# An image loaded and its statistics taken inside the filter stage; the next statistics taken inside the local convolution

## The reference, cut to what matters

```python
def _gn(v, G=8, eps=1e-05):
    g = v.reshape(B_, H_, W_, G, C_ // G)
    m = jnp.mean(g, axis=(1, 2, 4), keepdims=True)
    s = jnp.var(g, axis=(1, 2, 4), keepdims=True)
    return ((g - m) / jnp.sqrt(s + eps)).reshape(v.shape)

x = x + _L0_conv_ref(_gn(x), L0_conv_h0, L0_conv_numerators, L0_conv_denumerator)   # long filters, by FFT
x = x + _L1_conv_ref(_gn(x), ...)                                                   # 8x8 patches, large products
x = x + _L2_conv_ref(_gn(x), L2_conv_filters, L2_conv_bias)                         # 3x3 convolution
x = x + _L3_conv_ref(_gn(x), L3_conv_h0, L3_conv_numerators, L3_conv_denumerator)   # long filters again
```

## Time and profile before

| what | us |
|---|---|
| three runs: lowest, median, highest | 3507.69, 3509.49, 3510.06 |
| the profiled execution, its own time | 3497.7 |
| its span, first to last instruction | 3495.9 |
| TensorE busy | 3244.6 (93%) |
| VectorE busy | 1568.7 (45%) |
| ScalarE busy | 1680.7 (48%) |
| POOL busy | 1257.6 (36%) |

### The profile page before, as it was taken

The page is one execution under the profiler, slowest core; times in us unless marked ns, Lnnn a source line. Parts: engine busy times, 40 slices in busy tenths (PEclk is TensorE's granted clock), DMA queues, the critical chain, the costliest instruction groups (busy, mean ns, idle before and its releaser), DMA issues. The chain is left out here.

```text
span 3495.9 us, 82613 instructions
## 1 busy us (share of the span) xinstructions
PE 3244.6 (93%) x37272; PEld 2672.4 (76%) x37272; DVE 1568.7 (45%) x1926; ACT 1680.7 (48%) x1763; POOL 1257.6 (36%) x1018
## 2 busy tenths in 40 slices
PE   7999999589998699999899999999989997799998
PEld 6999998379998566666688776666668773489998
DVE  6787877411111434444765444344665444411112
ACT  3666665356553344444554434444454440355551
POOL 6888886055552102222440001222271000165550
PEclk9999999899999899999999999999999998899999
DMA  0333334787777321222133331222222344777776
GB/s 18 114 116 118 122 122 140 215 209 197 198 196 183 106 94 66 79 73 75 70 109 97 109 121 62 83 73 73 73 73 73 91 126 87 176 204 202 203 202 163
DMA packets 259721, 428.86 MB, mean 123 GB/s; under 512 B 28263, under 2 KB 106601, under 8 KB 257897
## 3 DMA queue, kind: packets, MB, share of 16 engines
q1 hardware_dynamic: 244346, 396.86, 38.9%
q10 hardware_dynamic: 15024, 26.72, 2.4%
HBM read 306.07 MB, written 113.77 MB: 120 GB/s over the span
## 5 line engine op out<-in xcount | busy, mean ns | idle before, releaser
L138 PE MATMUL m_bank<-xn,w 128*128 128x512 f32 x1536 | 619.2, 403 | 31.8 <-DVE m_store L1597 11.7
L139 PE MATMUL m_bank<-xn,w 128*128 128x512 f32 x1536 | 603.1, 393 | 0.0
L140 PE MATMUL m_bank<-xn,w 128*128 128x512 f32 x1536 | 602.8, 392 | 0.0
L774 PE MATMUL c_acc<-c_shifted,filt 128*32 128x256 f32 (+8 forms) x11264 | 457.2, 317 | 9.5 <-issue 9.4
L774 PEld LDWEIGHTS c_acc<-c_shifted,filt 128*32 128x32 f32 x11264 | 442.7, 159 | 20.3 <-issue 16.9
L568 POOL TENSOR_TENSOR filt<-filt 64x1408 f32<-64x1408 f32 x64 | 259.6, 4056 | 473.1 <-DMA filt<-filters_dram 473.1
L581 ACT ACTIVATE filt<-filt 64x2048 f32<-64x2048 f32 (+3 forms) x256 | 422.6, 1754 | 14.3 <-DMA filt<-filters_dram 10.6
L138 PEld LDWEIGHTS m_bank<-xn,w 128*128 128x128 f32 x1536 | 291.3, 190 | 172.9 <-issue 76.0
L129 ACT ACTIVATE w<-raw_weights 128x2048 fp32r<-128x2048 f32 x96 | 373.0, 3886 | 103.3 <-PE m_bank L140 102.0
L133 DVE TENSOR_TENSOR w<-raw_weights,w 128x2048 fp32r<-128x2048 f32 x86 | 334.0, 3883 | 159.0 <-ACT w L129 159.0
L140 PEld LDWEIGHTS m_bank<-xn,w 128*128 128x128 f32 x1536 | 291.1, 190 | 62.9
(11 more groups left out here) (182 smaller groups left out, 6763.7 us busy)
## 6 DMA issues: line engine op xcount, KB each, us to landing
c_shifted<-spectrum_dram SPq DMA_DIRECT2D x256, 270.0 KB, 3.9
filters_dram<-f_stage SPq DMA_DIRECT2D x128, 512.0 KB, 3.6
filt<-filters_dram SPq DMA_DIRECT2D x240, 256.0 KB, 4.7
raw_weights<-in_L_conv_Wq SPq DMA_DIRECT2D x16, 2048.0 KB, 8.7
raw_weights<-in_L_conv_Wk SPq DMA_DIRECT2D x16, 2048.0 KB, 8.6
raw_weights<-in_L_conv_Wv SPq DMA_DIRECT2D x16, 2048.0 KB, 8.6
m_qf<-in_L_conv_Wout SPq DMA_DIRECT2D x128, 256.0 KB, 3.9
spectrum_dram<-c_shifted SPq DMA_DIRECT2D x116, 136.0 KB, 2.4
```

The source lines that it names most:

```text
L138: pe.matmul(out, w[0], x[0], start=first, stop=False)
L139: pe.matmul(out, w[0], x[1], start=False, stop=False)
L140: return pe.matmul(out, w[1], x[0], start=False, stop=last)
L774: mm = nc.tensor.matmul(acc[k % 2][phase][32 * s:32 * s + 32, 0:B, LAGS * kb:HALF], filt[:, k, phase, :, :, 4 * kb + s].rearrange("p j c - ...
```

## The change

In the filter stage, the tiles `den` to `rec` and `spec` no longer have memory of their own: they lie in the image's tile of layer 0 and in the spare tile (`raw_weights`). When the last unit's spectrum is complete (`spec_ready`), SP loads the image into that tile, behind the stores of the last pair's `jp` 0, and VectorE takes the 32 `bn_stats` after its last work on lags. The tables `ident`, `average`, `fwd_w` are loaded by SP at the head of the filter stage. The eight stores of the last pair's `jp` 1 are issued in the next program, four by SP and four by ScalarE, and nothing waits for them at the end of the filter stage.

In layer 0, TensorE begins with the sum over partitions, with two channels transposed between the two sums and two after the second. ScalarE issues its four stores, takes a root of a constant (`warm`), and issues the eight loads of the first two filter groups one by one after its row copies 5 to 12 (counted from 0), with a wait for all filter stores ahead of the first.

In the local convolution, VectorE takes the `bn_stats` of layer 1's image: those of one image of the four after steps 6, 10 and 14, and those of the last after the loop. `local_conv` loads `average` and `fwd_w` for layer 1 at the end of SP's program, and its `ident` is passed on. In layer 1, SP issues the first filter loads ahead of all else.

Images, tables and the `stored` semaphores belong to two outer allocations now (`a_`, `e_`), each of which ends with a clear and a barrier of its own.

```diff
+def store_filters(eng, scratch, stage, stored, pair, jp, piece):
+
+    n = GROUPS // 8
+    return eng.dma_start(scratch["filters"][n * piece:n * piece + n, :, pair, jp].rearrange("g p n -> p g n"),
+                         stage[:, jp, n * piece:n * piece + n].rearrange("p g m k s -> p g (m k s)")).then_inc(stored[jp], 16)
...
+        ident_0, average, fwd_w, stats = tables
+        held = image[:].rearrange("p b w c -> p (b w c)")
+        size = DEEP * 8 * PAIRS
+        den, sq, straight, crossed = (held[:, 2 * size * n:2 * size * (n + 1)].rearrange("p (s f t n) -> p s f t n", s=DEEP, f=8, t=2)
+                                      for n in range(4))
+        mag, rec = (held[:, size * n:size * (n + 1)].rearrange("p (s f n) -> p s f n", s=DEEP, f=8) for n in range(8, 10))
...
+        spec = spare[:].rearrange("p a r n -> p (a r n)").rearrange("p (k c n f) -> p k c n f", k=2, c=2, n=PAIRS)
...
+            sp.dma_start(ident_0[:], const["ident"]).then_inc(tables_in, 16)
+            sp.dma_start(average[:], const["average"]).then_inc(tables_in, 16)
+            sp.dma_start(fwd_w[:], const["fwd_w"]).then_inc(tables_in, 16)
...
-            for jp in range(2):
-                for piece in range(PIECES):
-                    store(UNITS // 2 - 1, jp, piece)
-            for jp in range(2):
-                sp.wait_ge(stored[jp], 16 * PIECES * UNITS // 2)
+            for piece in range(PIECES):
+                store(UNITS // 2 - 1, 0, piece)
+            sp.wait_ge(spec_ready, UNITS)
+            for b in range(B):
+                sp.dma_start(image[:, b], io["x"][b]).then_inc(image_in[b], 16)
+            sp.wait_ge(tables_in, 48)
...
+            for b in range(B):
+                dve.wait_ge(image_in[b], 16)
+                image_stats(nc, image, stats, b).then_inc(stats_ready, 1)
+            dve.wait_ge(stats_ready, B)
...
+def image_stats(nc, image, stats, b):
+    for g in range(8):
+        op = nc.vector.bn_stats(stats[:, 8 * b + g], image[:, b, :, 2 * g:2 * g + 2])
+    return op
...
+    LAST_PAIR, FETCH_AT = 7, 5
...
-            if source is not None:
-                for b in range(B):
-                    sp.dma_start(image[:, b], source[b]).then_inc(image_in[b], 16)
-            sp.dma_start(ident[:], const["ident"]).then_inc(consts_in, 16)
-            sp.dma_start(average[:], const["average"]).then_inc(consts_in, 16)
-            sp.dma_start(fwd_w[:], const["fwd_w"]).then_inc(consts_in, 16)
+            if staged is not None:
+                stage, stored = staged
+                for at in range(4):
+                    store_filters(sp, scratch, stage, stored, LAST_PAIR, 1, at)
+            else:
+                for k in range(EARLY):
+                    for q in range(4):
+                        load_filters(sp, filt, scratch, layer, k, k, q).then_inc(filt_in[k], 16)
...
-            for i in range(4):
-                turn_channel(i)
-            pe.wait_ge(stats_ready, 1)
             nc.tensor.matmul(tot.rearrange("p (n s) -> p n s", s=2), average[:],
                              stats[:].rearrange("p n (s k) -> p n s k", k=3)[:, :, :, 1], start=True, stop=True).then_inc(sum_ready, 1)
+            turn_channel(0)
+            turn_channel(1)
             pe.wait_ge(mean_ready, 1)
             pe.wait_ge(spread_ready, 1)
             nc.tensor.matmul(tot, average[:], spread[:].rearrange("p n s -> p (n s)"), start=True, stop=True).then_inc(sum_ready, 1)
+            turn_channel(2)
+            turn_channel(3)
...
-            if source is not None:
-                act.wait_ge(image_in[B - 1], 16)
-            for k in range(EARLY):
-                for q in range(4):
-                    load_filters(act, filt, scratch, layer, k, k, q).then_inc(filt_in[k], 16)
+            if staged is not None:
+                stage, stored = staged
+                for at in range(4, 8):
+                    store_filters(act, scratch, stage, stored, LAST_PAIR, 1, at)
+            act.wait_ge(zeroed, 1)
+            nc.scalar.activation(warm[:], eps[:], ACT.Sqrt)
             act.wait_ge(var_ready, 1)
-            act.wait_ge(zeroed, 1)
             nc.scalar.activation(std[:], var[:], ACT.Sqrt, bias=eps[:, 0:1]).then_inc(std_ready, 1)
...
+                if staged is not None and FETCH_AT <= v < FETCH_AT + 4 * EARLY:
+                    if v == FETCH_AT:
+                        for jp in range(2):
+                            act.wait_ge(stored[jp], 16 * 8 * (LAST_PAIR + 1))
+                    k, q = divmod(v - FETCH_AT, 4)
+                    load_filters(act, filt, scratch, layer, k, k, q).then_inc(filt_in[k], 16)
...
+            sp.dma_start(average_2[:], const["average"]).then_inc(tables_in, 16)
+            sp.dma_start(fwd_w[:], const["fwd_w"]).then_inc(tables_in, 16)
+            sp.wait_ge(tables_in, 32)
...
+            def take_stats(b):
+                dve.wait_ge(moved, 4 * b + 4)
+                image_stats(nc, image, stats_2, b).then_inc(image_ready, 1)
+
             for t in range(16):
...
+                if t % 4 == 2 and t > 4:
+                    take_stats(t // 4 - 1)
+            take_stats(B - 1)
+            dve.wait_ge(image_ready, B)
```

More of the change, by code:

```diff
@@ L140, in split_product, with build_filters @@
     return pe.matmul(out, w[1], x[0], start=False, stop=last)
-def build_filters(nc, io, scratch, const):
+def store_filters(eng, scratch, stage, stored, pair, jp, piece):
+    n = GROUPS // 8
+    return eng.dma_start(scratch["filters"][n * piece:n * piece + n, :, pair, jp].rearrange("g p n -> p g n"),
+                         stage[:, jp, n * piece:n * piece + n].rearrange("p g m k s -> p g (m k s)")).then_inc(stored[jp], 16)
+def build_filters(nc, io, image, spare, tables, stage, stored, scratch, const):
     UNITS, PAIRS = 16, 32
@@ L187, in build_filters @@
         far_ready, far_out = sem("far_ready"), sem("far_out")
-        stored = [sem(f"stored{k}") for k in range(2)]
+        tables_in, stats_ready = sem("tables_in"), sem("stats_ready")
+        image_in = [sem(f"image_in{b}") for b in range(B)]
         block = ctx.enter_context(nc.Block())
@@ L582, in lower_columns, with filtered_layer @@
                           scale=1.0 if column else -1.0)
-def filtered_layer(nc, layer, image, source, spare, filt, scratch, const, out_dram, tag):
+def filtered_layer(nc, layer, image, tables, staged, spare, filt, scratch, const, out_dram, tag):
     N_BATCHES = GROUPS // RING
@@ L609, in filtered_layer @@
         sb, ps, sem = allocators(nc, ctx, tag)
-        ident = sb("ident", [128, 128])
-        average = sb("average", [128, 128])
-        fwd_w = sb("fwd_w", [L, 2, 128])
+        ident, average, fwd_w, stats = tables
         inv_w = sb("inv_w", [128, 2, L])
         eps = sb("eps", [128, 1])
-        stats = sb("stats", [128, 32, 6])
+        warm = sb("warm", [128, 1])
         dev = sb("dev", [128, 32, 2])
@@ L635, in filtered_layer @@
         img = [a[:].rearrange("p (j g) t -> p j (g t)", j=4) for a in (*acc[0], *acc[1])]
-        image_in = [sem(f"image_in{b}") for b in range(B)]
-        consts_in, stats_ready, zeroed = sem("consts_in"), sem("stats_ready"), sem("zeroed")
+        zeroed = sem("zeroed")
         sum_ready, mean_ready, dev_ready, sq_ready = sem("sum_ready"), sem("mean_ready"), sem("dev_ready"), sem("sq_ready")
@@ L865, in _ @@
             nc.vector.memset(odd[:, :, :, 0:1], 0.0).then_inc(edge_set, 1)
-            for n in range(32):
-                b, g = n // 8, n % 8
-                if source is not None and g == 0:
-                    dve.wait_ge(image_in[b], 16)
-                op = nc.vector.bn_stats(stats[:, n], image[:, b, :, 2 * g:2 * g + 2])
-            op.then_inc(stats_ready, 1)
             sample = stats[:].rearrange("p n (s k) -> p n s k", k=3)
@@ L1716, in _, with local_conv @@
                     normalise(half, n)
-def local_conv(nc, io, image, scratch, const, tag):
+def local_conv(nc, io, image, tables, scratch, const, tag):
     with ExitStack() as ctx:
@@ L1871, in build @@
     }
-    build_filters(nc, io, scratch, const)
     with nc.sbuf_tensor("mean1", [128, B], F32) as mean, nc.sbuf_tensor("rstd1", [128, B], F32) as rstd:
         with nc.sbuf_tensor("raw_weights", [128, 2, 8, 512], F32) as raw:
-            with nc.sbuf_tensor("image0", [128, B, L, C], F32) as image:
+            with ExitStack() as ctx:
+                sb, ps, sem = allocators(nc, ctx, "a_")
+                image = sb("image0", [128, B, L, C])
+                tables = tables_tensors(sb)
+                stored = [sem(f"stored{k}") for k in range(2)]
+                with nc.sbuf_tensor("stage", [128, 2, GROUPS, 4, L // 8, 4], F32) as stage:
+                    build_filters(nc, io, image, raw, tables, stage, stored, scratch, const)
                 with filter_tensor(nc, "filt0") as filt:
-                    filtered_layer(nc, 0, image, io["x"], raw, filt, scratch, const, None, "c0_")
```

(10 more changed lines are left out.)

21 lines of the change are left out of this document (5 added, 16 removed).

## The result

The changed kernel takes 3471.89 us (median of 16 runs, 3461.57 to 3496.33); the kernel before, run beside it, took 3508.48 (16 runs, 3497.15 to 3527.39). The ratio is 0.990, 95% interval 0.988 to 0.992: 36.6 us less, by the interval 28 to 42. The forecast was 28.3 less. Ratios here leave out single executions more than 1.5% above the fastest of their kernel and aren't quotients of the medians; medians and ranges are over all executions.

What follows compares the result with a forecast made beforehand. Bound by two holes without engine work ahead of the layers' first row transforms; -27.0 + 5 - 8.5 + 1 + 1.2 = -28.3 us off 3509.5 gives 3481 us (chance 0.59), range 3473 to 3490.

Steps and rivals of the forecast that it cites:

- Head 0: From the filter stage's last matmul to layer 0's first row transform: that transform 27.0 us earlier (24.7 to 29.7).
- ScalarE's stores were late next: Head of layer 0: four stores and the table load hold the root until 629.05, 2.7 us after the variance.
- The cover of VectorE over the last unit: End of filter stage: VectorE's statistics end 1.7 us before ScalarE's last copy, so they cost nothing.
- Nothing held the next program: Boundary into layer 0: program begins at 623.0; rival that last stores hold it, losing 13 us, 3494, chance 0.06.
- the wait for all filter stores: ScalarE's queue at layer 0's sixth row copy: costs nothing, 3 us cover; rival that it is late, 3521, chance 0.02.
- Head 1: From the local convolution's start to layer 1's first row transform: that transform 8.5 us earlier.
- Rows 1: Layer 1, first row transform to first filter-group matmul: 1 us longer (0 to 3), filter loads being ahead in SP's queue.
- the wait at the fifth copy: Layer 1's row stage: fifth copy due at 2996.2 gets its landed store at about 2998, behind SP's filter loads.
- The clash in the row stage: Layer 0: filter loads meeting row stores cost 5 us; rival strict sharing, 8.5 there and 3 in layer 1, 3487, chance 0.2.
- SP's stores don't pace the whole stage: Layer 0's row stage: the prediction had SP's queue of row stores pace it, one copy per 1.30 us.
- The two barriers: Ends of the two outer allocations: 0.6 us each, 1.2 in all (0 to 1.7).
- the 11.8 us: Whole kernel before: median 11.8 us above the profiled execution; the forecast difference was taken off the median.

Runs made afterwards that it cites:

- e3: The changed kernel run again without an edit, for a second profile; 3469.94 us, ratio 0.9906 to the kernel before.
- e11: Changed kernel plus five edits: POOL's subtraction and waits, early loads in both layers, SP issuing all last stores, filter-stage subtraction moved; 3440.27 us, ratio 0.9799.
- e12: Changed kernel with e11's edits, but last stores divided between SP and ScalarE, layer 1's tiles at the old addresses; 3441.84 us, ratio 0.9838.

## Why the prediction came out so

**Right, by its steps.** Head 0: 27.0 us forecast, 28.1 measured (36.7 to 37.0 against 8.7 to 8.8). ScalarE's stores were late next, as said: the variance was there at 628.84, the root began at 631.16. The 2.3 us between are less than forecast (2.7), as a store took 0.92 us to issue (3.66 / 4) and not 1.11. The cover of VectorE over the last unit was 1.8 us (625.18 less 623.39), forecast 1.7. Nothing held the next program, and the wait for all filter stores cost nothing: in the profile of after the first load behind it was issued at 642.85, while the copy ahead was still running, and the next copy waited 0.29 us, for TensorE. Head 1: 8.5 forecast, 8.5 measured by the means (114.3 to 105.8). Rows 1: 1 forecast, 0.8 measured by the means (47.1 to 47.9), no more than the scatter (46.4 to 47.5 without the change, 45.8 to 48.7 with it); the wait at the fifth copy came as described.

**Mis-sized.** The clash in the row stage: 5 forecast, 2.4 measured (mean of rows 0: 47.5 without the change, 49.9 with it). The step that failed is "I take 5, above the middle, as the share is what a row store queues for". The share counts the time that packets took, not how much of it they only waited. The other number of the same rows, 200 GB/s for the loads against 340 for the image, was the better guide, if the engines had room for row stores inside packets that wait; the runs show the price, not this reason. Besides, SP's stores don't pace the whole stage, though the sum had it so: in the trace of before the first eleven row copies (660.31 to 674.39) waited for TensorE, and only the later ones for a landed store. The two barriers: 1.2 forecast, none seen beyond the scatter (from the way back to the next stage 39.0 to 41.1 us without the first barrier, 39.6 to 41.9 with it; from the way back to the end 41.7 to 42.7 without the second, 40.1 to 43.9 with it).

**Not forecast.** Loop 1, about 5 us longer, cause open. In the filter stage the mean end is 1.5 us later (622.0 to 623.5), with the one subtraction of 3.4 us in four profiles of nine. Those four end at 624.4 to 625.2, the other five at 622.2 to 623.0, the three of the old stage at 621.2 to 623.1, so most of the 1.5 is that subtraction. The prediction had nothing there.

**The sum.** With the measured terms -28.1 + 2.4 - 8.5 + 0.8 = -33.4 us; with loop 1 and the filter stage, +4.8 and +1.5, -27. Forecast -28.3; the medians say -36.6 (28 to 42) and -36.5. So the forecast landed near the sum of the stretches by errors that cancel, and the medians lie some 8 us beyond the forecast, just outside my range of -20 to -36. The two profiled executions of before, 3497.7 and 3502.2, lie 11 and 4 under the medians beside them (3508.5, 3506.5), whereas e3's, 3471.0, lies 1 above its own. The remaining difference is therefore probably in executions that left no trace. That the standing subtraction is in more of them before than after is possible, but argued, not shown. I had taken the difference off the median, and had read the 11.8 us between the profile and the median of before as an offset, and not as a sign that stretches of this kernel may jump between executions, as the mixer of the changed kernel does by 18 us.

## What to carry to other kernels

A stretch with no engine at work is worth its length when the work ahead of it can be moved under a stage that has room: both heads gave what the chain of waits said, within some 1 us. What moves into a busy DMA stage can cost much less than its busy share (here a quarter): test it with no load and with double the load, as the double one may be a gain. Before a difference of 1% is read from two profiles, compare the stretches that the change doesn't touch; when one of them jumps, look for a VectorE instruction with both inputs in SBUF beside a run of POOL instructions without gaps, and limit how long POOL can run on.

## What the runs showed of the hardware

A subtraction of VectorE with both inputs in SBUF can stand still through a whole run of POOL's two-input operations: 25.11 us in place of 3.8 beside some 17 of them (1732.41 to 1753.95), 33.38 beside some 24. In the filter stage one took 3.37 in place of 0.63 and ended at 40.73, 0.3 us after POOL ran out of work (40.45). This fence is the timeline of the changed kernel there:

```profile
36.96 1.44 POOL L540 TENSOR_TENSOR a_image<-a_image 128x256 f32<-128x256 f32 x2
...
37.36 3.37 DVE L133 TENSOR_TENSOR f_respread<-stage,f_respread 128x256 fp32r<-128x256 f32 x1
...
38.32 0.75 POOL L532 TENSOR_TENSOR a_image<-a_image 128x256 f32<-128x256 f32 x1
39.00 1.45 POOL L550 TENSOR_TENSOR raw_weights<-a_image 128x256 f32<-128x256 f32 x2
```

In another execution of the same program the same instruction, at the same place, took 0.63. The Trainium skill (SBUF — State Buffer, Who interferes with whom) says that a VectorE instruction with two inputs in SBUF contends with a GpSimd instruction that reads SBUF, and that the order of issue decides which of them is blocked. The traces agree on who contends, and in 120 of the 124 cases above on the order: only the POOL operation that had begun went first, and the next one waited, taking 4.7 to 5.0 us in place of 1.3. In the other four, POOL operations that began after the subtraction went ahead of it, 3, 17, 17 and 24 of them, up to the end of POOL's run. So VectorE needs no gap to get in, as e3 and e11 show; but where it has once been passed over, it stood until POOL's stream had one, and e12 shows such a stand cut short by making POOL wait.
